# Attention and routed experts on one core: the low halves of the attention weights stored inside the float32 weights, eight steps deep, with new places for the side bank's users

## The chip, the cores and the metric

The kernel runs on one core of one Trainium2 chip. The metric is the device time in microseconds of one execution, shown as the median of three runs (2865.32 us, from 2861.77 to 2865.99).

## The reference

The input x has 4 sequences of 2048 tokens with 256 features, 8192 tokens in all. Cut to what matters, the reference is:

```
xn = layernorm(x)
s  = attention(xn)        # second norm with gain, 8 heads of 64, one shared K and V head,
                          # q and k scaled to norm 4, softmax(q k') v, Wout, norm with gain
g  = silu(experts(xn))    # router 256 -> 8, best 2, capacity 2560 rows an expert,
                          # gelu(x w1 + b1) w2 + b2, 1024 hidden, weighted sum of the two
out = x + s * g
```

Matrix products need more accuracy than one bf16 product gives. The kernel splits their operands into a high and a low half of 16 bits and adds the partial products that matter.

## The kernel before

**Groups and steps.** Queries are taken in 16 groups of 512 tokens, four groups to a sequence. A group's attention takes 64 steps. In a step TensorE computes the scores of two heads against 128 keys (six matmuls, L640, into one of two PSUM pairs of banks), ScalarE takes the exponential of the 128x1024 block (`exponent`, L869), and VectorE makes the low halves of the weights (`low`, L1220). TensorE then multiplies the weights with V, for the high halves (L668, 32 matmuls) and the low halves (L679, 16 matmuls).

**The product buffers.** `arena` holds NP = 6 float32 blocks (`p_f32`). The high half of a weight is the upper 16 bits of its float32 (`p_top[..., 1]`), read where it lies with a step of two elements. The low halves have six contiguous bf16 blocks of their own (`p_lo`). The exponential of step n waits until step n - NP has been weighed, and the weighing is placed LAG = 5 steps behind the scores, two steps at a time.

**Slots.** Every engine's program is made from one list of slots, each an attention step or a piece of another stage. In each slot an engine first issues its main instruction and then those of the "side chains", small programs that say at which slot each piece of theirs stands (`clock.at`). Engines run in order, so a place in that list is a place in each engine's queue. `base[g]` is the slot in which group g's attention starts. The order is written out by hand in the tables `S_...`, `KV_AT`, `Q_AT`, `O_...` and `C_AT`.

**Side chains in the attention stages.** For each group the kernel prepares q (four tiles, `prepare_q`), keys and values of a group of a later sequence (`prepare_kv`), the statistics and the router's logits (`statistics`), and projects the finished heads with Wout (four tiles, `project_out`). Their results on TensorE all go through one PSUM bank, the side bank `banks[3]`: `Ring.take` makes each user wait until the one before it has been read out. The output projection's result is read out by VectorE at L1173 (`s_rows`), q's by ScalarE (L815 and L818, the second frees the bank), keys' and values' by ScalarE at L800, the logits' by VectorE at L966.

**Places in a group of 64 slots.** q stands at 14, 30, 46 and 62, the projections at 37, 45, 53 and 61, keys and values at 38. The logits' place moves by 24 slots from one group to the next and so falls on 1, 9, 17, ... of a group of 64.

**Around the experts.** Eight groups come first, then all experts (L694 and L708), then the other eight groups. In these last ones `combine` gathers the experts' rows, multiplies and adds the result to `out` with a DMA from `res`.

SyncE issues the loads, stores and DMA transposes, in slot order too.

Of the kernel before, what the change touches and what calls it, by code (L numbers as in the profile page):

```python
# [7 lines left out]
F32 = mybir.dt.float32  # L8
# [7 lines left out]
P = 128  # L16
GT = 4
# [3 lines left out]
MIN_NORM = 1e-12  # L21
BANK = 512

NP = 6
LAG = 5
BEHIND = 4


# [41 lines left out]
def build_program(nc, x, norm_g, Wq, Wkv, Wout, out_norm_g, wr, w1, b1, w2, b2, out):  # L70
# [88 lines left out]
    def steps_to(g):  # L159
# [6 lines left out]


    S_SHIFT, S_NORM, S_HI, S_LO, S_STORE, S_TURN, S_LOGITS = [
        [early] * BG + [late] * (NG - BG) for early, late in ((3, 5), (4, 7), (5, 9), (6, 11), (9, 12), (9, 15), (12, 26))]
    KV_AT = [12 + 6 * g for g in range(BG)]  # L170
    KV_AT += [base[g - BG] + 38 for g in range(BG, NG)]

    EARLY_K_TURN, EARLY_Q_TURN = 9, 11
    Q_AT = [12 + 6 * j for j in range(GT)]
# [6 lines left out]
    for t in range(NT):  # L181
        g, j = divmod(t, GT)
        if g in BY_PE:
            at = experts_at + 4 * j if g == XG else place["post", 0, 0] + 1 + 6 * j
            O_SPLIT.append(at + 1)
            O_TURN.append(at + 4)
            O_PROJECT.append(at + 7)
        else:
            O_SPLIT.append(base[g + 1] + 11 + 4 * j)
            O_TURN.append(base[g + 1] + 27)  # L190
            O_PROJECT.append(base[g + 1] + 37 + 8 * j)
    C_AT = [base[XG + 1] + 20 + 13 * t if t < EARLY else O_SPLIT[t] + 8 if t // GT in BY_PE else
            base[t // GT + 1] + 34 + 12 * (t % GT) for t in range(NT)]
    C_ORDER = sorted(range(NT), key=lambda t: C_AT[t])
# [26 lines left out]
    with ExitStack() as ctx:  # L221
# [80 lines left out]


        PAIR = 2 * BANK
        arena = sb("arena", [P, NP * PAIR * 6], mybir.dt.uint8)
        p_f32 = arena[:, 0:NP * PAIR * 4].bitcast(F32).rearrange("p (n c) -> p n c", n=NP)
        p_top = arena[:, 0:NP * PAIR * 4].bitcast(BF16).rearrange("p (n c t) -> p n c t", n=NP, t=2)
        p_lo = arena[:, NP * PAIR * 4:NP * PAIR * 6].bitcast(BF16).rearrange("p (n c) -> p n c", n=NP)
        h_hi = [arena[:, i * 8192:(i + 1) * 8192].bitcast(BF16).rearrange("p (f c) -> p f c", f=FC) for i in (0, 1)]
        h_lo = [arena[:, i * 8192:(i + 1) * 8192].bitcast(BF16).rearrange("p (f c) -> p f c", f=FC) for i in (2, 3)]  # L310
        w1_hi = [sb(f"w1_hi{i}", [P, DC, F], BF16) for i in range(2)]
# [5 lines left out]
        xgT = [cut(flat(att[(XG + 1) % 2], F16), i, [2 * DC, GP]) for i in range(2)]  # L317
        b2_rows = [cut(flat(vhl_row[1], F32), i, [D]) for i in range(2)]

        res = [cut(flat(w1_lo[1], F32), i, [D]) for i in range(2)]  # L320
        y_got = [cut(flat(w1_lo[0], F32), i, [TOP_K, D]) for i in range(2)]

        early_x = [cut(flat(att[g // 2], F32), g % 2, [GT, D]) for g in range(BG)]
# [71 lines left out]
        c_loaded = [sem(f"c_loaded{i}") for i in range(2)]  # L395
        y_gathered = [sem(f"y_gathered{i}") for i in range(2)]
        x_copied = sem("x_copied")
        out_stored = [sem(f"out_stored{i}") for i in range(2)]
        f_first, f_both, c_tanh, c_silu, c_times = [sem(n) for n in (
            "f_first", "f_both", "c_tanh", "c_silu", "c_times")]  # L400

# [45 lines left out]
        def _(engine):  # L447
# [197 lines left out]
            def weigh(n, turn):  # L645

                s = n % NP
                if turn:
                    pe.wait_ge(half_weighed, n - n % 2 + 2)
                else:  # L650
                    pe.wait_ge(weighed, n - n % 2)
                pe.wait_ge(exped, n + 1)
                if n == CUT:
                    pe.wait_ge(y_done, FG * GT)
                for i, g, h, kb in halves(n):
                    b, hh = g // BG, g * H + h
                    V, bank = vhl[b % 2], acc_banks[hh % 3]
                    pe.wait_ge(v_split, BG * b + kb // GT + 1)
                    if kb == 0:
                        pe.wait_ge(divided, hh - 2)  # L660
                for qb in range(GT):
                    at = qb * (DH + 1)
                    for width, of in ((DH + 1, 0), (DH, DH + 1)):
                        for i, g, h, kb in halves(n):
                            V, bank = vhl[g // BG % 2], acc_banks[(g * H + h) % 3]
                            rows = slice((i + turn) % 2 * DH, ((i + turn) % 2 + 1) * DH)
                            cols = slice(i * BANK + qb * P, i * BANK + (qb + 1) * P)
                            nc.tensor.matmul(bank[:, at:at + width], p_top[rows, s, cols, 1],  # L668
                                             V[rows, kb, of:of + width],
                                             start=(kb == 0 and qb == 0 and turn == 0 and of == 0), stop=False,  # L670
                                             skip_group_check=True)
                pe.wait_ge(lowed, n + 1)
                for qb in range(GT):
                    at = qb * (DH + 1)
                    for i, g, h, kb in halves(n):
                        V, bank = vhl[g // BG % 2], acc_banks[(g * H + h) % 3]
                        rows = slice((i + turn) % 2 * DH, ((i + turn) % 2 + 1) * DH)
                        cols = slice(i * BANK + qb * P, i * BANK + (qb + 1) * P)
                        t = nc.tensor.matmul(bank[:, at:at + DH + 1], p_lo[rows, s, cols], V[rows, kb, 0:DH + 1],  # L679
                                             start=False, stop=(kb == KB - 1 and turn == 1), skip_group_check=True)  # L680
                t.then_inc(weighed if turn else half_weighed, 1)

# [56 lines left out]
        def _(engine):  # L739
# [68 lines left out]
            def prepare_q(t_id):  # L808
                g, j = divmod(t_id, GT)
                yield from clock.at(Q_AT[t_id])  # L810
                bank = where["q", t_id]
                act.wait_ge(q_projected, t_id + 1)
                act.wait_ge(q_scaled, t_id)
                act.wait_ge(s_rstd, g + 1)
                nc.scalar.activation(q_f[:, :, :].rearrange("p h n -> p (h n)"), bank, ACT.Copy,  # L815
                                     scale=rstd[:, g, 1, j:j + 1]).then_inc(q_copied, 1)
                act.wait_ge(q_lo, t_id)
                nc.scalar.activation(q_n[:, :, :].rearrange("p h n -> p (h n)"), bank, ACT.Square,  # L818
                                     scale=rstd[:, g, 1, j:j + 1]).then_inc(q_squared, 1)
                yield from clock.at(Q_AT[t_id] + 6)  # L820
                act.wait_ge(q_scaled, t_id + 1)
                act.wait_ge(q_turned_early, min(t_id, GT))
                act.wait_ge(q_stored, 16 * (t_id - GT) if t_id > GT else 0)
                cast(q_his, q_n[:, :, :].rearrange("p (a b) n -> p a b n", b=2)).then_inc(q_hi, 1)
                if t_id < GT:
                    yield from clock.at(Q_AT[t_id] + EARLY_Q_TURN)
                    act.wait_ge(q_turned_early, t_id + 1)
                    cast(qT[0][:, :, j * P:(j + 1) * P], where["qT", t_id].bitcast(F16).rearrange(
                        "p (h c) -> p h c", h=H)).then_inc(qT_copied, 1)
# [66 lines left out]
        def _(engine):  # L896
# [223 lines left out]
                                        ALU.subtract).then_inc(k_lo, 1)  # L1120

            def prepare_q(t_id):
                yield from clock.at(Q_AT[t_id] + 1)
                dve.wait_ge(q_squared, t_id + 1)
                nc.vector.tensor_reduce(q_small[:, 0, :], q_n[:, :, :], AX, ALU.add).then_inc(q_sum, 1)
                dve.wait_ge(q_sum, t_id + 1)
                nc.vector.tensor_scalar(q_small[:, 1, :], q_small[:, 0, :], SCALE ** 2 / (SCALE ** 3),  # L1127
                                        MIN_NORM ** 2 / SCALE ** 3, ALU.mult, ALU.max).then_inc(q_var, 1)
                yield from clock.at(Q_AT[t_id] + (5 if t_id < GT else 4))
                dve.wait_ge(q_rstd, t_id + 1)  # L1130
                nc.vector.tensor_tensor(q_n[:, :, :], q_f[:, :, :],
                                        q_small[:, 2, :].unsqueeze(2).to_broadcast([P, H, DH]),
                                        ALU.mult).then_inc(q_scaled, 1)
                yield from clock.at(Q_AT[t_id] + (7 if t_id < GT else 8))
                dve.wait_ge(q_hi, t_id + 1)
                nc.vector.tensor_tensor(q_los, q_n[:, :, :].rearrange("p (a b) n -> p a b n", b=2), q_his,
                                        ALU.subtract).then_inc(q_lo, 1)
# [38 lines left out]
            def combine(t_id):  # L1176
# [11 lines left out]
                if t_id < EARLY:  # L1188
# [1 line left out]
                dve.wait_ge(s_ready, t_id + 1)  # L1190
                dve.wait_ge(o_rstd, t_id + 1)
                dve.wait_ge(c_silu, i + 1)
                dve.wait_ge(out_stored[i % 2], 16 * (i // 2))
                nc.vector.scalar_tensor_tensor(out=res[i % 2], in0=w, scalar=half_rstd[:, t_id:t_id + 1], in1=s,
                                               op0=ALU.mult, op1=ALU.mult).then_inc(c_times, 1)

            def divide(hh):
# [18 lines left out]
            def low(n):  # L1216
                dve.wait_ge(exped, n + 1)
                dve.wait_ge(weighed, n - NP + 1)
                c = columns(n)
                nc.vector.tensor_tensor(p_lo[:, n % NP, c], p_f32[:, n % NP, c], p_top[:, n % NP, c, 1],  # L1220
                                        ALU.subtract).then_inc(lowed, 1)

            def rest_of_hidden(fg, f):
# [30 lines left out]
        def _(engine):  # L1254
# [49 lines left out]
                power(k_small[:, 2, :], k_small[:, 1, :], GT).then_inc(k_rstd, 1)  # L1304

            def prepare_q(t_id):
                yield from clock.at(Q_AT[t_id] + 2)
                pool.wait_ge(q_var, t_id + 1)
                power(q_small[:, 2, :], q_small[:, 1, :], H).then_inc(q_rstd, 1)

# [5 lines left out]
            def combine(t_id):  # L1316
# [12 lines left out]
                yield from clock.at(C_AT[t_id] + 15)  # L1329
                pool.wait_ge(x_copied, 16 * NG)  # L1330
                pool.wait_ge(c_times, i + 1)
                nc.gpsimd.dma_start(out_tiles[t_id], res[i % 2], accum_op=ALU.add).then_inc(out_stored[i % 2], 16)  # L1332

            def main(kind, a, b):
                pass
# [6 lines left out]
        def _(engine):  # L1342
# [48 lines left out]
            def prepare_kv(g):  # L1391
                b, gi = divmod(g, BG)
                if g < BG:
                    return
                yield from clock.at(KV_AT[g] - (34 if g > BG else 22))
                sp.wait_ge(s_stored[g % 2], 16 * (g // 2 + 1))
                sp.wait_ge(q_projected, GT * (g - BG + 1))
                sp.wait_ge(kv_projected, g)
# [16 lines left out]
            def prepare_q(t_id):  # L1415
                g, j = divmod(t_id, GT)
                if g == 0:
                    return
                yield from clock.at(Q_AT[t_id] + 9)
                sp.wait_ge(q_lo, t_id + 1)  # L1420
                nc.sync.dma_start(q_tiles[t_id], qhl[:, :, :, :, :].rearrange("p a k b n -> p (a k b n)")
                                  ).then_inc(q_stored, 16)
# [77 lines left out]
            def main(kind, a, b):  # L1500
# [5 lines left out]
                zero_rows(i) for i in range(NZERO)] + [move_rows(t) for t in range(NT)] + [load_routed(fg) for fg in range(FG)] + [project_out(t) for t in range(NT)] + [store_rows(fg) for fg in range(FG)] + [  # L1506
                copy_x(g) for g in range(NG)] + [
                combine(t) for t in C_ORDER])
            for i in range(2):
                sp.wait_ge(out_stored[i], 16 * NT // 2)  # L1510


_INS = ["L0_attn_x", "L0_attn_norm_g", "L0_attn_Wq", "L0_attn_Wkv", "L0_attn_Wout", "L0_attn_out_norm_g",
# [18 lines left out]
```

## Time and profile before

| | |
|---|---|
| median of 3 runs | 2865.32 us (2861.77 to 2865.99) |
| the profiled execution, its own time | 2859.94 us |
| its span, first to last instruction | 2858.2 us |
| TensorE matmuls busy | 2607.0 us, 91% of the span |
| VectorE busy | 2015.9 us, 71% |
| ScalarE busy | 1742.5 us, 61% |
| GpSimd busy | 673.4 us, 24% |
| mean granted TensorE clock | 0.976 |

Times in a view are from the span's start. The busy time of an engine counts its own instructions only. Idle time before an instruction is put down to what ended it; "issue" means that no semaphore explains it. The matmuls' ends are modelled, so that a busy TensorE is not one at its peak. Some matmul records are missing.

### The profile page before, as it was taken

How to read it: one execution, taken by the hardware profiler on the slowest of the kernel's cores; microseconds unless marked ns; L12 is line 12 of the kernel's file. 1: busy time of each engine (PE TensorE's matmuls, PEld its weight loads, DVE VectorE, ACT ScalarE, POOL GpSimd, SP SyncE). 2: the span in 40 equal slices, each digit the busy share in tenths (PEclk: the TensorE clock that was granted, in tenths of full speed). 3: DMA queues.
4: the chain of work that ended last, by engine and by line, in shares of the span. 5: the costliest groups of instructions: out<-in, count | busy, mean ns of one | idle time of the engine just before them, and what ended most of it. 6: DMA issues, size and time to landing. Idle time of an engine off the chain costs nothing. (4 is left out here: it accounts for less than half of the span.)

```text
span 2858.2 us, 136218 instructions
## 1 busy us (share of the span) xinstructions
PE 2607.0 (91%) x63045; PEld 1839.0 (64%) x63045; DVE 2015.9 (71%) x3013; ACT 1742.5 (61%) x2259; POOL 673.4 (24%) x492
## 2 busy tenths in 40 slices
PE   4898989888798999999999999999999899999995
PEld 3666666655466666666676666776666666666674
DVE  5888879889787874333433434348888899889985
ACT  6776757665565655554545545447766667667673
POOL 3111111111677500000000000003243434434313
PEclk8999999999899999999999999999999999999997
DMA  3455556322654522323323322211443434334412
GB/s 100 107 118 132 130 124 152 87 63 66 177 144 142 128 59 60 106 55 96 106 68 97 96 63 69 51 44 41 80 83 80 84 78 91 72 73 85 71 45 39
DMA packets 405611, 254.50 MB, mean 89 GB/s; under 512 B 291433, under 2 KB 369201, under 8 KB 404785
## 3 DMA queue, kind: packets, MB, share of 16 engines
q1 hardware_dynamic: 383536, 203.82, 29.4%
q0 software_dynamic: 21504, 41.96, 6.8%
q8 instruction: 494, 8.09, 1.2%
q14 instruction: 77, 0.62, 0.1%
HBM read 65.32 MB, written 121.63 MB: 65 GB/s over the span
## 5 line engine op out<-in xcount | busy, mean ns | idle before, releaser
L1220 DVE TENSOR_TENSOR arena<-arena 128x1024 bf16<-128x1024 f32 (+1 forms) x1032 | 1223.5, 1210 | 217.5 <-ACT arena L869 215.4
L869 ACT ACTIVATE arena<-pair 128x1024 f32<-128x1024 f32 (+1 forms) x1032 | 1041.6, 1016 | 419.5 <-PE pair L640 416.0
L668 PEld LDWEIGHTS bank<-vhl,arena 64*128 64x128 bf16 x32768 | 752.7, 95 | 288.5 <-issue 64.2
L640 PE MATMUL pair<-qT,kT 64*128 64x512 f16 x6144 | 864.3, 381 | 34.5 <-ACT arena L869 23.2
L668 PE MATMUL bank<-vhl,arena 64*128 64x64 bf16 (+1 forms) x32768 | 842.2, 191 | 44.8 <-issue 42.7
L679 PE MATMUL bank<-vhl,arena 64*128 64x65 bf16 x16384 | 616.4, 191 | 43.3 <-issue 27.8
L876 ACT ACTIVATE h_f<-pair,b1T 128x512 f32<-128x512 f32 x320 | 218.8, 684 | 379.6 <-PE pair L694 379.1
L679 PEld LDWEIGHTS bank<-vhl,arena 64*128 64x128 bf16 x16384 | 412.5, 95 | 54.9 <-issue 34.5
L1269 POOL TENSOR_TENSOR q_small<-q_small,minus_half 128x8 f32<-128x8 f32 x64 | 144.6, 2260 | 1272.7 <-DVE q_small L1127 1272.3
L708 PE MATMUL bank<-w_hl,arena 128*128 128x256 bf16 x3840 | 426.9, 273 | 0.3
L708 PEld LDWEIGHTS bank<-w_hl,arena 128*128 128x128 bf16 x3840 | 375.3, 98 | 53.6 <-DVE att L1236 2.0
L1226 DVE TENSOR_TENSOR arena<-h_f,arena 128x512 bf16<-128x512 f32 x320 | 221.4, 692 | 264.7 <-ACT arena L743 264.1
L694 PE MATMUL pair<-att,w_hi 128*128 128x512 f16 x1280 | 382.6, 381 | 2.5 <-DMA att<-routed_rows 2.5
L640 PEld LDWEIGHTS pair<-qT,kT 64*128 64x128 f16 x6144 | 247.2, 94 | 211.9 <-issue 66.7
L1236 DVE TENSOR_TENSOR att<-bank,vhl 128x256 f32<-128x256 f32 x160 | 67.8, 424 | 263.4 <-PE bank L708 261.9
L694 PE MATMUL pair<-att,w_lo 128*128 128x512 f16 x640 | 243.6, 381 | 0.0
L694 PEld LDWEIGHTS pair<-att,w_hi 128*128 128x128 bf16 x1280 | 125.4, 98 | 145.5 <-DMA att<-routed_rows 2.7
L743 ACT ACTIVATE arena<-h_f 128x512 bf16<-128x512 f32 x320 | 201.5, 630 | 10.1
L1325 POOL DMA_INDIRECT w_lo<-expert_rows,gather_from x128 | 186.7, 1458 | 81.4 <-DVE c_work L1182 50.8
L1297 POOL DMA_INDIRECT routed_rows<-xT_out,scatter_to x128 | 168.8, 1319 | 83.2 <-issue 32.4
L815 ACT ACTIVATE q_f<-bank,rstd 128x512 f32<-128x512 f32 x63 | 43.3, 688 | 129.9 <-PE bank L566 129.5
L1269 POOL TENSOR_TENSOR half_rstd<-o_small,minus_half 128x1 f32<-128x1 f32 x64 | 39.6, 618 | 349.3 <-DVE o_small L1165 349.0
(190 smaller groups left out, 1596.5 us busy)
## 6 DMA issues: line engine op xcount, KB each, us to landing
routed_rows<-h_f SPq DMA_DIRECT2D x80, 256.0 KB
expert_rows<-att SPq DMA_DIRECT2D x40, 512.0 KB, 2.8
raw<-in_L_ffn_w SPq DMA_DIRECT2D x32, 512.0 KB, 4.6
q_rows<-qhl SPq DMA_DIRECT2D x60, 256.0 KB
o_rows<-o_hl SPq DMA_DIRECT2D x56, 256.0 KB
xn_rows<-s_hl SPq DMA_DIRECT2D x16, 512.0 KB, 3.3
xT_out<-xn_rows SPq DMA_DIRECT2D x64, 128.0 KB
out<-in_L_attn_x SPq DMA_DIRECT2D x16, 512.0 KB, 4.2
```

Source lines behind the costliest of these rows:

```text
L640: t = nc.tensor.matmul(into, kT[g // BG % 2][rows, k_part, keys], qT[g % 2][rows, h // 2 * 2 + q_part, :], start=(k_part + q_part == 0), s ...
L668: nc.tensor.matmul(bank[:, at:at + width], p_top[rows, s, cols, 1], V[rows, kb, of:of + width], start=(kb == 0 and qb == 0 and turn == 0 a ...
L679: t = nc.tensor.matmul(bank[:, at:at + DH + 1], p_lo[rows, s, cols], V[rows, kb, 0:DH + 1], start=False, stop=(kb == KB - 1 and turn == 1) ...
L694: t = nc.tensor.matmul(bank, w[e % 2][:, c, cols], xgT[fg % 2][:, kind, :], start=(n == 0), stop=(n == 3 * DC - 1))
L708: t = nc.tensor.matmul(bank[:, 0:D], h[fg % 2][:, f, cols], w2_hl[e % 2][:, f, at:at + D], start=(f == 0 and h is h_hi and at == 0), stop= ...
L743: return nc.scalar.activation(o, i, ACT.Copy)
L869: nc.scalar.activation(p_f32[:, n % NP, columns(n)], pairs[n % 2][:, columns(n)], ACT.Exp).then_inc(exped, 1)
L876: nc.scalar.activation(h_f32[k % 2], lent[k % 4], ACT.Gelu_apprx_tanh, bias=b1T[:, e * FC + f:e * FC + f + 1]).then_inc(gelued, 1)
L1220: nc.vector.tensor_tensor(p_lo[:, n % NP, c], p_f32[:, n % NP, c], p_top[:, n % NP, c, 1], ALU.subtract).then_inc(lowed, 1)
L1226: nc.vector.tensor_tensor(h_lo[fg % 2][:, f, :], h_f32[k % 2], h_hi[fg % 2][:, f, :], ALU.subtract).then_inc(h_rest, 1)
L1269: return nc.gpsimd.tensor_tensor(o, i, minus_half[:, 0:n], ALU.pow)
L1325: nc.gpsimd.indirect_dma_start(y_got[i % 2][:, k, :], None, expert_rows, bass.IndirectOffsetOnAxis(gather_from[k][:, t_id:t_id + 1], 0)).t ...
```

## The change

Seven edits are made together.

1. `p_lo` is gone. `low` writes the low half of each weight into the lower 16 bits of the weight's own float32 (`p_top[..., 0]`), and the low-half matmuls read it there, with a step of two elements.
2. NP goes from 6 to 8 and LAG from 5 to 7.
3. The side bank's users move: keys and values from slot 38 of the group to 22, the last three projections from 45, 53 and 61 to 40, 53 and 56, the logits two slots later.
4. In `prepare_q` ScalarE makes its second read of the bank (the square) one slot later than the first, and the steps on VectorE, GpSimd and SyncE behind it follow one slot later.
5. SyncE issues the load of xT for keys and values at slot 2 of the group, and not at 4.
6. `res` has four buffers and four semaphores in place of two.
7. With LAG, each of the two attention stages gets two more slots, in which only weighing is left, and the weighing starts two slots later.

```diff
-NP = 6
-LAG = 5
+NP = 8
+LAG = 7
...
-        [early] * BG + [late] * (NG - BG) for early, late in ((3, 5), (4, 7), (5, 9), (6, 11), (9, 12), (9, 15), (12, 26))]
+        [early] * BG + [late] * (NG - BG) for early, late in ((3, 5), (4, 7), (5, 9), (6, 11), (9, 12), (9, 15), (12, 28))]
...
-    KV_AT += [base[g - BG] + 38 for g in range(BG, NG)]
+    KV_AT += [base[g - BG] + 22 for g in range(BG, NG)]
...
-            O_PROJECT.append(base[g + 1] + 37 + 8 * j)
+            O_PROJECT.append(base[g + 1] + (37, 40, 53, 56)[j])
...
-        arena = sb("arena", [P, NP * PAIR * 6], mybir.dt.uint8)
+        arena = sb("arena", [P, NP * PAIR * 4], mybir.dt.uint8)
...
-        p_lo = arena[:, NP * PAIR * 4:NP * PAIR * 6].bitcast(BF16).rearrange("p (n c) -> p n c", n=NP)
...
-        res = [cut(flat(w1_lo[1], F32), i, [D]) for i in range(2)]
+        res = [cut(flat(w1_lo[1], F32), i, [D]) for i in range(4)]
...
-        out_stored = [sem(f"out_stored{i}") for i in range(2)]
+        out_stored = [sem(f"out_stored{i}") for i in range(4)]
...
-                        t = nc.tensor.matmul(bank[:, at:at + DH + 1], p_lo[rows, s, cols], V[rows, kb, 0:DH + 1],
+                        t = nc.tensor.matmul(bank[:, at:at + DH + 1], p_top[rows, s, cols, 0], V[rows, kb, 0:DH + 1],
...
+                if g:
+                    yield
...
-                yield from clock.at(Q_AT[t_id] + 6)
+                yield from clock.at(Q_AT[t_id] + (6 if g == 0 else 7))
...
-                yield from clock.at(Q_AT[t_id] + 1)
+                yield from clock.at(Q_AT[t_id] + (1 if t_id < GT else 2))
...
-                yield from clock.at(Q_AT[t_id] + (5 if t_id < GT else 4))
+                yield from clock.at(Q_AT[t_id] + 5)
...
-                yield from clock.at(Q_AT[t_id] + (7 if t_id < GT else 8))
+                yield from clock.at(Q_AT[t_id] + (7 if t_id < GT else 9))
...
-                dve.wait_ge(out_stored[i % 2], 16 * (i // 2))
-                nc.vector.scalar_tensor_tensor(out=res[i % 2], in0=w, scalar=half_rstd[:, t_id:t_id + 1], in1=s,
+                dve.wait_ge(out_stored[i % 4], 16 * (i // 4))
+                nc.vector.scalar_tensor_tensor(out=res[i % 4], in0=w, scalar=half_rstd[:, t_id:t_id + 1], in1=s,
...
-                nc.vector.tensor_tensor(p_lo[:, n % NP, c], p_f32[:, n % NP, c], p_top[:, n % NP, c, 1],
+
+                nc.vector.tensor_tensor(p_top[:, n % NP, c, 0], p_f32[:, n % NP, c], p_top[:, n % NP, c, 1],
...
-                yield from clock.at(Q_AT[t_id] + 2)
+                yield from clock.at(Q_AT[t_id] + (2 if t_id < GT else 3))
...
-                nc.gpsimd.dma_start(out_tiles[t_id], res[i % 2], accum_op=ALU.add).then_inc(out_stored[i % 2], 16)
+                nc.gpsimd.dma_start(out_tiles[t_id], res[i % 4], accum_op=ALU.add).then_inc(out_stored[i % 4], 16)
...
-                yield from clock.at(KV_AT[g] - (34 if g > BG else 22))
+                yield from clock.at(base[g - BG] + (2 if g > BG else 16))
...
-                yield from clock.at(Q_AT[t_id] + 9)
+                yield from clock.at(Q_AT[t_id] + 10)
...
-            for i in range(2):
-                sp.wait_ge(out_stored[i], 16 * NT // 2)
+            for i in range(4):
+                sp.wait_ge(out_stored[i], 16 * NT // 4)
```

## Rows read from the trace of the kernel before

**Rows 1.** Busy time by stretch: before, during and after the experts

```profile
core 0: us, PE busy (x) PEld busy (x) DVE busy (x) ACT busy (x) POOL busy (x), PEclk, DMA share, GB/s
67.00:1059.00 992.00, 874.33 (x28527) 627.68 (x28526) 833.03 (x1218) 635.09 (x742) 309.44 (x212) 0.97 0.47 116
1059.00:1912.00 853.00, 848.37 (x5890) 572.21 (x5887) 322.27 (x527) 432.80 (x671) 2.15 (x4) 1.00 0.28 76
1912.00:2812.00 900.00, 836.45 (x28153) 603.38 (x28152) 804.77 (x1102) 622.38 (x760) 323.77 (x238) 0.99 0.36 73
```

**Rows 2.** TensorE's waits: waiter, releaser, us in total, times, longest

```profile
PE bank L668 <- issue: 42.7, 64, 3.0
PE bank L566 <- DVE s_rows L1173: 38.8, 19, 5.6
PE bank L679 <- issue: 27.8, 44, 1.4
PE pair L640 <- ACT arena L869: 23.2, 28, 9.6
PE bank L679 <- DVE arena L1220: 14.5, 29, 1.7
PE bank L534 <- DVE s_rows L1173: 8.8, 6, 2.3
...
PE bank L601 <- DVE s_rows L1173: 1.7, 2, 1.0
PE bank L511 <- DVE s_rows L1173: 1.3, 1, 1.3
```

**Rows 3.** Timeline around a projection and the q behind it

```profile
2328.85 1.48 PE L617 MATMUL bank<-wo_hl,att 128*128 128x256 bf16 x12
...
2333.68 0.47 DVE L1173 SCALAR_TENSOR_TENSOR s_rows<-bank,o_small,out_g 128x256 f32<-128x256 f32 x1
...
2334.22 0.81 PE L566 MATMUL bank<-wq_hi,xT 128*128 128x512 bf16 x2 [2.39 <-DVE s_rows L1173]
...
2336.67 1.41 PE L640 MATMUL pair<-qT,kT 64*128 64x512 f16 x6
```

**Rows 4.** Ten stretches at half clock: the first, the last, their sum

```profile
269.40:272.80 3.40, 3.09 (x10) 0.50 0.84 192
...
2477.80:2481.20 3.40, 3.40 (x36) 0.51 0.68 142
sum 37.40, PE 35.46; mean PE 3.55
```

**Rows 5.** Timeline: the scores of two steps in a row, undisturbed

```profile
402.24 0.82 PE L640 MATMUL pair<-qT,kT 64*128 64x512 f16 x6
...
403.63 0.81 PE L640 MATMUL pair<-qT,kT 64*128 64x512 f16 x6
```

**Rows 6.** Groups of instructions: busy us, mean ns of one, idle before

```profile
L1220 DVE TENSOR_TENSOR arena<-arena 128x1024 bf16<-128x1024 f32 (+1 forms) x1032 | 1223.5, 1210 | 217.5 <-ACT arena L869 215.4 <-PE bank L679 0.4 <-issue 0.3
L869 ACT ACTIVATE arena<-pair 128x1024 f32<-128x1024 f32 (+1 forms) x1032 | 1041.6, 1016 | 419.5 <-PE pair L640 416.0
...
L668 PEld LDWEIGHTS bank<-vhl,arena 64*128 64x128 bf16 x32768 | 752.7, 95 | 288.5 <-issue 64.2 <-PE bank L679 4.4
...
L679 PEld LDWEIGHTS bank<-vhl,arena 64*128 64x128 bf16 x16384 | 412.5, 95 | 54.9 <-issue 34.5 <-DVE arena L1220 18.8
...
L1194 DVE SCALAR_TENSOR_TENSOR w_lo<-c_work,half_rstd,s_xin 128x256 f32<-128x256 f32 x32 | 15.5, 485 | 3.5 <-DVE c_work L1186 1.0
...
L1046 DVE TENSOR_TENSOR w_hl<-w_hl,w_lo 128x512 f32<-128x512 f32 x1 | 0.7, 678 | 0.0
```

**Rows 7.** Busy time by stretch: the groups 10 and 14

```profile
2132.50:2251.20 118.70, 107.44 (x3566) 77.10 (x3560) 105.52 (x152) 80.36 (x104) 48.76 (x36) 0.99 0.44 85
...
2597.00:2705.60 108.60, 102.29 (x3520) 73.88 (x3514) 101.60 (x142) 77.63 (x96) 47.37 (x34) 1.00 0.37 72
```

**Rows 8.** The page's DMA queues: packets, MB, share of 16 engines

```profile
q8 instruction: 494, 8.09, 1.2%
```

**Rows 9.** ScalarE's waits: the two longest that VectorE ended

```profile
ACT c_work L860 <- DVE c_work L1182: 42.4, 34, 4.7
ACT qhl L743 <- DVE q_n L1131: 28.6, 28, 3.6
```

## The prediction

> **What bounds the kernel now.** I read the busy time by stretch first. The experts (853 us) keep TensorE busy for 848.37 us, and no edit touches their work. The two attention stretches, 992 and 900 us, are where the change acts. TensorE is busy there for 874.33 and 836.45 us, VectorE for 833.03 and 804.77 us, ScalarE for little over 620 to 635 us [rows 1]. So TensorE leads, VectorE follows closely, and ScalarE has room.
>
> An undisturbed step takes 1.39 us, from one step's first score matmul to the next one's [rows 5]. VectorE needs 1.21 us of it for the low halves and ScalarE 1.02 us for the exponential [rows 6]. 64 such steps are 89 us, while group 14 took 108.6 us and group 10 118.7 us [rows 7]: the rest is side work and waits.
>
> The waits of TensorE are the next view [rows 2]. The side bank is waited for until VectorE has read out a projection: 38.8 + 8.8 + 1.7 + 1.3 = 50.6 us. "issue" takes 42.7 + 27.8 = 70.5 us. Waits for low halves take 14.5 us, for exponentials 23.2 us. The timeline shows how one side bank wait arises: the projection's matmuls end at 2330.33 us, VectorE works through older work in its queue and ends the read-out at 2334.15 us, and q's matmuls, one slot behind, start at 2334.22 after 2.39 us idle [rows 3].
>
> Such a wait costs a second time. Right behind it q's six matmuls take from 2334.22 to 2336.67, 2.45 us, and the scores after them show 1.41 us where 0.82 is usual [rows 3, 5]. I looked for stretches at half clock and for what stood at their start: ten of them, 37.4 us together, stand at a side bank wait, with a granted clock of 0.5, the lower of the two levels (1.2 and 2.4 GHz) [rows 4].
>
> **Part by part.**
>
> *The side bank's users (edit 3).* A wait of this kind is on average 38.8 / 19 = 2.0 us, behind a slot of 1.39 us, so the bank is free some 3.4 us after the projection's last matmul. Where one slot lay between a projection and its successor (45 to 46, 61 to 62, 37 to 38), now at least three lie there (40 to 46, 56 to 62, 37 to 40), 4.2 us. The average fits, the longest (5.6 + 1.39 = 7.0 us) does not. New neighbours three slots apart (37 and 40, 53 and 56) can wait too. I leave 6 us and take -44.6. Bounds: -50.6, all gone, and -25, half of it comes back at the new neighbours. Keys and values leave slot 38; their nine VectorE instructions stood at 39 and 43, just ahead of the read-out at 45, and now stand at 23 and 27, where none waits behind them. That is in the same term.
>
> *The clock.* Half speed for 37.4 us loses at most 18.7 us. In [rows 3] the loss was 2.45 us against about 1.28 (half) for q alone. Some of it lay where ScalarE or VectorE were late anyway. I take -13, with bounds 0 and -18.7. The Trainium skill (TensorE: Matmul & The Clock Gate, HAM oscillation) reckons throttled time times one half, which gives 18.7 us here and a sum 6 us lower; the trace agrees with the half speed itself, since q's matmuls took twice as long.
>
> *Eight deep, seven behind (edit 2).* The distance from an exponential to the step that frees its buffer is one slot more than LAG before and after, so ScalarE gains nothing. VectorE does: a low half may be two slots later before TensorE waits. What that can return is the 14.5 us of waits for low halves [rows 2]. I take half, -7, bounds 0 and -14.5. The 23.2 us for exponentials stay, since ScalarE's distance is the same as before.
>
> *Low halves in place (edit 1).* The instruction count is the same. TensorE loads weights with a step of two elements already for the high halves: 95 ns, and 95 ns for the contiguous low halves [rows 6]. So the loads cost 0. VectorE's write is new: bf16 with a step of two, over its own input. Nearest row below: an in-place f32 TENSOR_TENSOR, 678 ns for 512 [rows 6], which continues to 1210 for 1024 at 1.04 ns an element, the present rate; so nothing more. Nearest above: the slowest VectorE form per element, 485 ns for 256; less the same fixed 146 ns it is 1.32 ns an element, 0.29 us more for 1024. I take 0, because a float32 write steps over the same bytes at the usual rate. Both ends stay for the range.
>
> *Longer fill and drain (edit 7).* Two more steps in two stages have only scores on TensorE (0.82 us) while VectorE sets 1.21 us: 4 x 0.4 = 1.6 us, rounded to +2, bounds 0 and 4. The weighing left over at the ends is work moved, not added.
>
> *q's chain (edit 4)* adds no instruction. The bank is held one slot longer, and the next user stands two or more slots away. Behind ScalarE's square wait VectorE's reduction, GpSimd's power and SyncE's store, all one slot later. SyncE's eight transposes of qT stay at slot 58 and q's last store moves to 56, still eight slots ahead of the next group. 0. *xT's load and keys (edits 3, 5)*: SyncE issues four transposes two slots earlier, the k store at 29 and the two kT transposes at 32 of the group, right behind the eight of the projection at 27, where before they stood at 45 and 48. They queue; the projection at 37 could be late by a DMA. The bytes are the same, K is needed groups later. 0, bounds 0 and +5. *Four res buffers (edit 6)*: no wait of VectorE names the store, so 0.
>
> *What is late next.* TensorE without pauses draws instructions faster, and VectorE must keep up. Part of the "issue" time comes back: 70.5 us over about 1,900 us of attention is 3.7%; where 31 side bank waits covered such a delay, I put +5 (0 to +15). VectorE: after the change the attention would last about 1892 - 52 = 1840 us with 1637.8 us busy [rows 1], 89%. Group 14 ran at 101.6 of 108.6, 93.6%, with little waiting [rows 7]; so it can, but in the crowded groups (10: 105.5 busy, floor 105.5 / 0.936 = 112.7 us against the 111 I would hope for) some comes back: +6 (0 to +20).
>
> *Sum*: -44.6 - 13 - 7 + 2 + 5 + 6 = -51.6 us. The profiled execution took 2859.94 us, 5.4 less than the median of 2865.32; 2859.9 - 51.6 = 2808.3 in its terms, and about 2814 in those of the median.
>
> **The rivals.**
>
> *A, forecast:* the pauses go and most of it is kept, 2790 to 2835. Chance 0.52.
>
> *B, VectorE takes the place.* The waits move from the side bank to low halves and to ScalarE, which already waits for VectorE for 42.4 + 28.6 us [rows 9]; a deeper buffer lets VectorE fall further behind and makes these longer. For it: VectorE is at 105.5 of 118.7 us in group 10. Against it: only 14.5 us of waits for low halves now. If crowding costs 30 us in place of 6 and the clock returns half, the sum is about -21: 2844. Chance 0.17.
>
> *C, instructions take the place.* TensorE gets its instructions in 494 packets, 8.09 MB, with the other engines' [rows 8]; each "issue" wait stands inside a run of matmuls that wait for no semaphore. If 25 of the 50 us come back there, with the clock's gain halved, it is about -25: 2840. Chance 0.07. The Trainium skill (Runtime: NRT & Kernel Launch, Instruction fetch mechanics) holds this fetch to be mostly hidden, by which this rival would have no room; the 70.5 us of this trace speak against it.
>
> *D, slower: the strided write.* At +0.29 us VectorE is busy for 1032 x 0.29 = 299 us more, 1937 us in attention, above its present 1892 us; at the 93.6% of group 14 it needs 2069 us. Between them lies about +110 us: 2975. It decides from 1840 x 0.936 = 1722, so (1722 - 1638) / 1032 = 0.08 us a step. A smaller slowing, or a transposing queue on SyncE that makes projections late in every group, ends nearer. Chance 0.12, over all of that.
>
> *E, more:* low-half waits, clock and side bank give all they hold and the rows behind absorb it: -50.6 - 18.7 - 14.5 + 2 = -82: 2784 and below. Chance 0.09. *F, nothing:* what is saved at one bank user is waited for at the next: within 0.2%. Chance 0.03.
>
> **How the numbers follow.** 0.2% of the time, 5.7 us, is about what a measurement of this kernel can tell from no change. Faster by more: A, C, E and nearly all of B, 0.84. Within: F and the ends of B and D, 0.05. Slower: the rest of D, 0.11. The range 2775 to 2850 holds A, most of B and C, and the near part of E, and leaves D out; A's own is 2790 to 2835.
>
> **What would show it.** Side bank waits on `s_rows` under 10 us in all; fewer stretches at half clock, mean clock from 0.976 to about 0.983; low halves still at 1.21 us; waits for low halves under 15 us; "issue" between 70 and 85 us; group 10 near 111 us and group 14 unchanged near 108; TensorE busy less by what the clock gives. The prediction fails if the low halves take over 1.29 us, if ScalarE's waits for VectorE double, or if the waits reappear at 37 to 40 and 53 to 56.

## The result

The changed kernel takes 2959.68 us (median of 4 runs, 2953.06 to 2968.85), the kernel before 2865.65 us beside it: a ratio of 1.033, 95% interval 1.0294 to 1.0365. It is slower by 3.3%, where 1.8% faster was forecast. The profiled execution has a span of 2962.4 us; the mean granted clock fell from 0.976 to 0.964.

Busy time by stretch of the changed kernel, before, during and after the experts, with columns as in [rows 1]:

```profile
67.00:1127.00 1060.00, 884.55 (x28441) 628.76 (x28441) 890.35 (x1216) 638.03 (x742) 466.48 (x212) 0.94 0.45 109
1127.00:1983.00 856.00, 850.96 (x5985) 574.60 (x5978) 322.56 (x528) 432.66 (x671) 2.16 (x4) 1.00 0.28 76
1983.00:2914.00 931.00, 837.07 (x28099) 603.12 (x28098) 865.89 (x1103) 620.48 (x761) 530.87 (x238) 0.99 0.36 70
```

The experts are as they were. The two attention stretches are longer by 68 and 31 us. TensorE and ScalarE have the same instructions. VectorE is busy for 118 us more, now more than TensorE in both stretches, and GpSimd is busy for 997 us where it was 633.

Groups of instructions of the changed kernel that answer to [rows 6] (L1222 was L1220). L1271 is GpSimd's power for q, which raises the squared lengths to the power of -0.5; L1327 is the gather of the experts' rows in `combine`:

```profile
L1222 DVE TENSOR_TENSOR arena<-arena 128x1024 bf16<-128x1024 f32 (+1 forms) x1032 | 1358.1, 1365 | 82.8 <-ACT arena L870 80.6
...
L667 PEld LDWEIGHTS bank<-vhl,arena 64*128 64x128 bf16 x32768 | 750.8, 95 | 291.4 <-issue 63.5
...
L1271 POOL TENSOR_TENSOR q_small<-q_small,minus_half 128x8 f32<-128x8 f32 x64 | 233.1, 3642 | 1259.7 <-DVE q_small L1128 1259.5
...
L678 PEld LDWEIGHTS bank<-vhl,arena 64*128 64x128 bf16 x16384 | 412.1, 95 | 37.8 <-issue 35.9
...
L1327 POOL DMA_INDIRECT w_lo<-expert_rows,gather_from x128 | 336.1, 2626 | 78.7 <-DVE c_work L1183 48.7
```

A low half takes 1365 ns, not 1210. (Both are means over 1032 instructions, 16 of which have 512 elements; those of 1024 alone take 1374 and 1219 ns.) Loading the weights with a step of two costs nothing, 95 ns as before. Unforeseen is GpSimd: its power for q takes 3642 ns, its gathers 2626. In the kernel before these two groups, and VectorE's wait for the power, were:

```profile
L1269 POOL TENSOR_TENSOR q_small<-q_small,minus_half 128x8 f32<-128x8 f32 x64 | 144.6, 2260 | 1272.7 <-DVE q_small L1127 1272.3
L1325 POOL DMA_INDIRECT w_lo<-expert_rows,gather_from x128 | 186.7, 1458 | 81.4 <-DVE c_work L1182 50.8 <-issue 30.7
```

```profile
DVE q_n L1131 <- POOL q_small L1269: 10.1, 8, 3.8
```

TensorE's waits in the changed kernel, against [rows 2]:

```profile
PE pair L639 <- ACT arena L870: 138.4, 92, 11.6
PE bank L667 <- issue: 36.4, 56, 1.9
PE bank L678 <- issue: 30.3, 42, 1.8
PE bank L616 <- DMA att<-o_rows: 26.9, 7, 14.3
PE pair L639 <- DMA qT<-q_rows: 13.1, 7, 5.6
...
PE bank L616 <- DVE s_rows L1174: 8.2, 12, 1.4
...
PE bank L678 <- DVE arena L1222: 0.7, 2, 0.4
```

The side bank waits are nearly gone, as forecast (8.2 us in this row, about 12 in all), and so are those for low halves. In their place the scores wait 138.4 us for exponentials, and the waits for DMAs grow from 12.6 to 40.0 us (26.9 and 13.1 here; 10.6 and 2.0 before). The new places alone don't make the latter: with them and contiguous low halves (experiment 6) they are 15.8 us. Who holds ScalarE, and who holds VectorE behind it, the waits of these two engines tell (against [rows 9]):

```profile
ACT qhl L742 <- DVE q_n L1132: 143.1, 55, 13.9
...
ACT c_work L861 <- DVE c_work L1183: 60.9, 41, 4.7
ACT o_hl L742 <- DVE att L1214: 39.0, 14, 6.4
```

```profile
DVE q_n L1132 <- POOL q_small L1271: 120.2, 41, 13.9
DVE arena L1222 <- ACT arena L870: 80.6, 66, 5.2
```

So there is a chain: VectorE waits for GpSimd's power, ScalarE for VectorE's scaled q, the next exponential stands behind that in ScalarE's queue, and TensorE waits for it. One link of it in the changed kernel's timeline:

```profile
2067.22 0.17 DVE L1128 TENSOR_SCALAR q_small<-q_small 128x8 f32<-128x8 f32 x1
2067.30 3.90 DVE L1222 TENSOR_TENSOR arena<-arena 128x1024 bf16<-128x1024 f32 x3
2067.48 5.22 POOL L1271 TENSOR_TENSOR q_small<-q_small,minus_half 128x8 f32<-128x8 f32 x1 [0.88 <-DVE q_small L1128]
...
2072.74 0.69 DVE L1132 TENSOR_TENSOR q_n<-q_f,q_small 128x512 f32<-128x512 f32 x1 [1.53 <-POOL q_small L1271]
...
2073.46 0.63 ACT L742 ACTIVATE qhl<-q_n 128x512 f16<-128x512 f32 x1 [1.93 <-DVE q_n L1132]
```

While three low halves run back to back for 3.90 us, the power, started at 2067.48, doesn't end; it ends at 2072.70, 1.5 us after the last of them, and VectorE stands idle for that time. It is as if the power got on only once VectorE paused.

Groups 10 and 14 (against [rows 7]), and the groups 5 and 6, in which GpSimd scatters the rows and which took 139.1 and 124.6 us before:

```profile
2209.10:2331.50 122.40, 107.32 (x3564) 76.61 (x3558) 112.89 (x152) 79.79 (x103) 69.70 (x36) 0.99 0.41 81
2687.50:2802.30 114.80, 103.94 (x3538) 74.89 (x3532) 108.70 (x142) 77.35 (x95) 70.56 (x33) 0.99 0.34 72
```

```profile
678.30:839.00 160.70, 113.75 (x3556) 80.28 (x3551) 124.75 (x169) 81.76 (x93) 113.98 (x51) 0.89 0.42 115
839.00:995.20 156.20, 113.72 (x3560) 80.83 (x3556) 103.41 (x125) 75.02 (x84) 135.57 (x75) 0.88 0.43 122
```

The groups 5 and 6 alone lose 53 us, and there it is for the most part not the power's own length. Of VectorE's 120.2 us of waits for it, 73.0 us are eight waits of over 4 us, all between 760 and 1047 us, six of them in these two groups, and each time the power itself took 1.7 us. It started late, because GpSimd's queue had fallen behind with scatters (1955 ns on average against 1319 before, the longest 10.05 us against 2.00). The end of the longest of these waits:

```profile
888.90 0.96 POOL L1299 DMA_INDIRECT routed_rows<-xT_out,scatter_to  x1 [0.31 <-issue]
889.88 1.68 POOL L1271 TENSOR_TENSOR q_small<-q_small,minus_half 128x8 f32<-128x8 f32 x1
...
891.59 0.69 DVE L1132 TENSOR_TENSOR q_n<-q_f,q_small 128x512 f32<-128x512 f32 x1 [13.91 <-POOL q_small L1271]
```

From 878.77 us on, with VectorE idle, GpSimd issues nine scatters of 0.96 us each, and only then comes to the power. Beside low halves just before, they took up to 5.88 us. So the chain has two causes in GpSimd, a slow power and slow scatters and gathers ahead of it.

### The profile page after: what moved, and what is told of

Same layout as the page of the kernel before. It is cut to its first block and busy times, and to the rows that moved or that the text cites. A ratio compares the mean times of both kernels' runs of the same rounds, so it can differ in the third digit from the quotient of the medians.

```text
span 2962.4 us, 136209 instructions
## 1 busy us (share of the span) xinstructions
PE 2621.8 (89%) x63045; PEld 1843.5 (62%) x63045; DVE 2134.2 (72%) x3013; ACT 1743.4 (59%) x2259; POOL 1037.4 (35%) x492
## 5 line engine op out<-in xcount | busy, mean ns | idle before, releaser
L1222 DVE TENSOR_TENSOR arena<-arena 128x1024 bf16<-128x1024 f32 (+1 forms) x1032 | 1358.1, 1365 | 82.8 <-ACT arena L870 80.6
L639 PE MATMUL pair<-qT,kT 64*128 64x512 f16 x6144 | 867.4, 384 | 156.3 <-ACT arena L870 138.4
L1271 POOL TENSOR_TENSOR q_small<-q_small,minus_half 128x8 f32<-128x8 f32 x64 | 233.1, 3642 | 1259.7 <-DVE q_small L1128 1259.5
L1327 POOL DMA_INDIRECT w_lo<-expert_rows,gather_from x128 | 336.1, 2626 | 78.7 <-DVE c_work L1183 48.7
L1299 POOL DMA_INDIRECT routed_rows<-xT_out,scatter_to x128 | 250.2, 1955 | 70.5 <-ACT arena L870 33.6
L1271 POOL TENSOR_TENSOR half_rstd<-o_small,minus_half 128x1 f32<-128x1 f32 x64 | 57.9, 905 | 250.2 <-DVE o_small L1166 249.9
L1132 DVE TENSOR_TENSOR q_n<-q_f,q_small 128x512 f32<-128x512 f32 x64 | 44.3, 692 | 120.3 <-POOL q_small L1271 120.2
```

What stands on the lines that cost most here:

```text
L639: t = nc.tensor.matmul(into, kT[g // BG % 2][rows, k_part, keys], qT[g % 2][rows, h // 2 * 2 + q_part, :], start=(k_part + q_part == 0), s ...
L1222: nc.vector.tensor_tensor(p_top[:, n % NP, c, 0], p_f32[:, n % NP, c], p_top[:, n % NP, c, 1], ALU.subtract).then_inc(lowed, 1)
L1271: return nc.gpsimd.tensor_tensor(o, i, minus_half[:, 0:n], ALU.pow)
L1299: nc.gpsimd.indirect_dma_start(routed_rows, bass.IndirectOffsetOnAxis(scatter_to[k][:, t:t + 1], 0), moving[t % 4], None).then_inc(rows_sc ...
L1327: nc.gpsimd.indirect_dma_start(y_got[i % 2][:, k, :], None, expert_rows, bass.IndirectOffsetOnAxis(gather_from[k][:, t_id:t_id + 1], 0)).t ...
```

## The experiments

Ratios are to the kernel before on the same chip. "P" and the other letters are the theories that each text names.

**1. The write in place alone, and all but the write.** The first puts edit 1 into the kernel before:

```diff
-nc.vector.tensor_tensor(p_lo[:, n % NP, c], p_f32[:, n % NP, c], p_top[:, n % NP, c, 1], ...
+nc.vector.tensor_tensor(p_top[:, n % NP, c, 0], p_f32[:, n % NP, c], p_top[:, n % NP, c, 1], ...
```

> The kernel before with edit 1 alone: low halves written into the float32 weights, still six buffers and five steps behind, every place as before. Theory P (the price of the low halves carries the loss): VectorE's low halves take 1.36 to 1.37 us in place of 1.21, VectorE is busy for some 118 us more, and without the side bank's gain the time is 2950 to 3020 us. Rival Q (the moved places and the deeper lag carry the loss, by SyncE's and GpSimd's queues; the longer low halves lie in VectorE's slack): the low halves take 1.36 us too, but the time stays within 2865 to 2890 us.

Measured: 3010.53 us, ratio 1.052 (1.0477 to 1.0562). Low halves 1361 ns, GpSimd's power 2999 ns, side bank waits 88.3 us in all where they were 50.6. The group of low halves and that of the power:

```profile
L1219 DVE TENSOR_TENSOR arena<-arena 128x1024 bf16<-128x1024 f32 (+1 forms) x1032 | 1360.8, 1361 | 170.1 <-ACT arena L868 163.3 <-issue 6.2
...
L1268 POOL TENSOR_TENSOR q_small<-q_small,minus_half 128x8 f32<-128x8 f32 x64 | 191.9, 2999 | 1220.4 <-DVE q_small L1126 1220.2
```

The second takes edit 1 out of the changed kernel. Eight buffers with contiguous blocks beside them would need 12 KiB more in each partition, so NP and LAG go back as well:

```diff
-NP = 8
-LAG = 7
+NP = 6
+LAG = 5
-nc.vector.tensor_tensor(p_top[:, n % NP, c, 0], ...
+nc.vector.tensor_tensor(p_lo[:, n % NP, c], ...
```

> The changed kernel with the low halves back in contiguous blocks of their own, and so with six buffers and five steps behind; the side bank's places, q's chain, the loads and the four res buffers as changed. Theory P: low halves at 1.21 us, side bank waits under 15 us, 2800 to 2840 us, faster than before by 1 to 2%. Rival Q: 2880 us or more, with the exponentials late (over 100 us of waits of the score matmuls for them) as in the changed kernel.

Measured: 2826.14 us, ratio 0.9866 (0.9823 to 0.991), low halves 1211 ns, the power 2254 ns. Theory P holds: edit 1 carries the loss, the rest is a gain. Q falls. That NP and LAG went back too doesn't blur this: the six-deep kernel of experiment 5 (1.035) differs from this one in edit 1 alone.

**2. Is it the step, or writing over the input?** Both kernels have NP = 4 and LAG = 3, which leaves room to write the low halves with a step of two into a region of their own:

```diff
-nc.vector.tensor_tensor(p_lo[:, n % NP, c], p_f32[:, n % NP, c], ...
+nc.vector.tensor_tensor(p_two[:, n % NP, c, 0], p_f32[:, n % NP, c], ...
```

> The kernel before with four buffers and three steps behind, contiguous low halves: the partner of the next run, which needs more room a buffer. Only the duration of the low halves matters: 1.21 us. With less depth TensorE waits more for low halves; 2870 to 2960 us.

> As the run before it, four buffers and three steps behind, but the low halves are written with a step of two elements into a region of their own, not into their inputs. If the step is what costs, 1.36 us as in the changed kernel, and a time above its partner's by 60 us or more. If writing into the words that the same instruction reads is what costs, 1.21 us and its partner's time within 10 us. A value between says that both have a part.

Measured, one run each: 3007.98 us with contiguous low halves, 3114.22 us with the step. The group of low halves, first contiguous, then with the step:

```profile
L1220 DVE TENSOR_TENSOR arena<-arena 128x1024 bf16<-128x1024 f32 (+1 forms) x1032 | 1240.7, 1214 | 359.1 <-ACT arena L869 351.1 <-PE bank L679 3.5 <-issue 1.7
```

```profile
L1220 DVE TENSOR_TENSOR arena<-arena 128x1024 bf16<-128x1024 f32 (+1 forms) x1032 | 1384.3, 1361 | 321.2 <-ACT arena L869 315.6 <-PE bank L679 2.6 <-issue 0.5
```

1214 and 1361 ns: the step costs all of it, and writing over the input nothing. Four buffers were slower than expected (3008 us, outside the 2870 to 2960): TensorE then waits 279.5 us for low halves.

**3. VectorE's time, or GpSimd's turn?** Contiguous low halves cut into parts make VectorE as busy as the step does.

```diff
-nc.vector.tensor_tensor(p_lo[:, n % NP, c], p_f32[:, n % NP, c], ..., ALU.subtract).then_inc(lowed, 1)
+for at in range(c.start, c.stop, BANK):      # in the three-part kernel: 512, 256, 256
+    h = slice(at, at + BANK)
+    t = nc.vector.tensor_tensor(p_lo[:, n % NP, h], p_f32[:, n % NP, h], ..., ALU.subtract)
+t.then_inc(lowed, 1)
```

> The kernel before with each contiguous low-half instruction of 1024 cut into two of 512, which took 0.693 us each where they occur: 1.39 us a step, slightly more than the 1.36 us of the write with a step of two, and with no such write. Theory T (VectorE's time alone makes the loss): 3000 to 3040 us, close to the 3010.5 us of the in-place write in the same kernel, and GpSimd's power for q goes from 2.26 us towards 3 us too. Rival U (the write with a step of two harms others beside its own length, GpSimd above all): 2900 to 2960 us, and the power stays near 2.3 us.

Measured: 2888.75 us, ratio 1.0083 (1.0052 to 1.0113). Both ranges missed, for it wasn't the clean test that the text says: the two parts overlap at their ends, so that VectorE was busy with low halves for 1292.4 us, 0.067 us a step more, not 0.18. GpSimd's power took 2000 ns. The next run corrects the size:

> The kernel before with each contiguous low-half instruction cut into three, of 512, 256 and 256. Two parts added 0.067 us a step to VectorE's busy time (1.292 in place of 1.224 ms in all), so three add some 0.134 us and VectorE is as busy as with the write in place (about 2135 us), but GpSimd can take its turn between the parts. If VectorE's time alone made the loss of the in-place write (3010.5 us), this ends near 2990 to 3020 us. If GpSimd's turns made a good part of it, 2900 to 2940 us, with the power for q near 2.0 us.

Measured: 2923.81 us, ratio 1.0181 (1.0147 to 1.0214), low halves busy 1357.5 us as with the step, the power 1989 ns. VectorE's time by itself costs 1.8%, while the step in the same kernel costs 5.2%. The gathers took 1502 ns here, against 2747 with the step.

The other way round, the in-place low halves of experiment 1 cut in two:

> The kernel with the in-place write alone (3010.5 us), its low-half instruction cut into two of 512. VectorE works longer, by about 0.067 us a step, 69 us in all, and GpSimd gets a turn between the two. If VectorE's time is what counts, 3050 to 3080 us. If GpSimd being kept out is what counts, the time falls although VectorE has more to do: 2940 to 2990 us, and the power for q falls from 3.0 us to about 2.2.

Measured: 2943.35 us, ratio 1.0231 (1.0195 to 1.0267). Its low halves and its power for q:

```profile
L1221 DVE TENSOR_TENSOR arena<-arena 128x512 bf16<-128x512 f32 x2048 | 1367.7, 746 | 179.2 <-ACT arena L868 173.7 <-issue 4.8
...
L1271 POOL TENSOR_TENSOR q_small<-q_small,minus_half 128x8 f32<-128x8 f32 x64 | 127.0, 1984 | 1267.6 <-DVE q_small L1126 1267.5
```

VectorE is as busy as uncut (1367.7 against 1360.8 us; no 69 us more), the power falls from 2999 to 1984 ns, and the time from 1.052 to 1.023. That is where contiguous parts with the same VectorE time stand (1.018; the intervals overlap). VectorE is busy for 71 to 73% of the span in all these kernels, and also with contiguous low halves in one piece, where the power takes 2275 ns (places alone, experiment 6). So neither the busy time nor the step alone makes the power slow, but a stepped write in one long piece. The gathers are another matter: cut in two they still take 2284 ns, so that the step has a part of its own in them.

**4. GpSimd out of q's chain.** In the changed kernel:

```diff
+nc.vector.reciprocal(q_small[:, 2, :], q_small[:, 1, :]).then_inc(q_rstd, 1)
-power(q_small[:, 2, :], q_small[:, 1, :], H).then_inc(q_rstd, 1)
```

> The changed kernel without GpSimd's power in q's chain: VectorE takes a reciprocal there, so that q is scaled by one over its squared length and not by one over the length. It costs VectorE 64 x 0.18 = 12 us and takes the wait for GpSimd (120 us in the changed kernel) out of its queue. If that wait carries the loss, 2890 to 2925 us, with waits of the score matmuls for exponentials under 70 us (138 in the changed kernel). If VectorE's own time carries it, 2960 to 2975 us.

Measured: 2902.1 us, ratio 1.0109 (1.0082 to 1.0137), against 1.033 with the power. The scores wait 76.4 us for exponentials (somewhat over the 70 forecast), not 138.4. The link counts, though gathers (2753 ns) and the other powers stay slow. The edit takes VectorE's wait away whichever its cause, the slow power or the scatters ahead of it, so it doesn't weigh the two.

**5. Time for q's chain, and the depth.** Two runs on the changed kernel. The first gives the steps behind the power two slots more:

```diff
-yield from clock.at(Q_AT[t_id] + 5)
+yield from clock.at(Q_AT[t_id] + (5 if t_id < GT else 7))
```

> The changed kernel with the steps of q behind GpSimd's power two slots later (VectorE's scaling at 7, ScalarE's cast at 9, VectorE's rest at 11, the store at 12, the transposes at 13). VectorE waited for that power 120 us in the changed kernel. If these waits cost time by themselves, they fall under 40 us and the time to 2900 to 2930 us. If GpSimd only gets its turn when VectorE pauses, the power takes longer instead and the time stays within 10 us of 2960 us.

Measured: 2968.76 us, ratio 1.036 (1.0328 to 1.0391). VectorE's wait for the power fell to 58.6 us, but the power took 4069 ns. The scores waited less for exponentials (93.2 us) and more for the transposes of qT (41.2 us against 13.1), and the side bank's users 27.6 us for read-outs against 11.6. Room at this place doesn't help, since what it saves is waited for elsewhere.

> The changed kernel with six buffers and five steps behind, low halves still in place. It tells what the two buffers more give once VectorE is the bound. Theory: depth lets VectorE fall behind without TensorE waiting for low halves, so this is slower than the changed kernel by 10 to 30 us, 2970 to 2990 us, with 40 us or more of waits for low halves. Rival: depth only moves the waits from the low halves to the exponentials, the same within 6 us of 2960 us.

Measured: 2963.36 us, ratio 1.035 (1.0314 to 1.0386), against 1.033 (1.0294 to 1.0365) with eight: no difference that these runs can tell. Waits for low halves are 66.3 us and not 0.7, those for exponentials 107.1 and not 138.4: the rival's reading, the depth mostly moves the wait.

**6. The places alone, and the changed kernel with cut low halves.** The first puts only the side bank's places into the kernel before (the load of xT stays at slot 4):

```diff
-(12, 26)
+(12, 28)
-KV_AT += [base[g - BG] + 38 ...
+KV_AT += [base[g - BG] + 22 ...
-O_PROJECT.append(base[g + 1] + 37 + 8 * j)
+O_PROJECT.append(base[g + 1] + (37, 40, 53, 56)[j])
```

> The kernel before with the side bank's places alone: keys and values at 22, projections at 37, 40, 53 and 56, logits two slots later; q's chain, xT's load at slot 4, two res buffers, six deep as before. Theory: the places carry all of the gain seen with everything but the in-place write (2826 us): 2820 to 2835 us. Rival: ScalarE's later square (q's chain) has a part, then 2840 to 2855 us.

Measured: 2815.49 us, ratio 0.982 (0.9786 to 0.9853), the fastest of all. The whole of TensorE's waits for the side bank after a projection:

```profile
PE bank L601 <- DVE s_rows L1173: 1.7, 2, 1.0
...
PE pair L640 <- DVE s_rows L1173: 1.4, 1, 1.4
PE bank L617 <- DVE s_rows L1173: 0.3, 1, 0.3
```

Against 2826.14 us with q's chain, xT's load and four res buffers as well, the intervals of the two ratios overlap; these other edits give nothing that the runs can tell.

> The changed kernel with its in-place low halves cut into two instructions of 512. Cut in the kernel with the in-place write alone, VectorE was as busy as before (1368 against 1361 us in the low halves) and the time fell by 67 us. If the same mechanism makes the changed kernel slow, 2880 to 2910 us, GpSimd's power for q near 2.0 us and VectorE's wait for it under 20 us (120 in the changed kernel). If the moved places or the depth make it slow, 2950 us or more. Even at best it stays above the places alone (2815 us), since VectorE still has 0.13 us a step more to do.

Measured over 10 runs: 2877.28 us, ratio 1.0025 (0.9997 to 1.0053), the power 1939 ns, waits for exponentials 78.1 us. VectorE's wait for the power is 31.7 us, not under 20; nearly all of it (30.7 us) comes with a power that started right behind another instruction of GpSimd, the longest four behind scatters. One more instruction in each step brings the changed kernel back to the time of the kernel before. Against the places alone (0.982) it is still 2 points slower, so it takes back some 60% of what the step costs.

## Why the prediction was wrong

**The step that failed** is "Low halves in place (edit 1)": "I take 0, because a float32 write steps over the same bytes at the usual rate." The run measured 1365 ns, 0.155 us more a step, or 0.13 us in VectorE's busy time (1358.1 against 1223.5 us). The bracket of 0 to 0.29 us held it, and rival D had the right place: it decides from 0.08 us a step, and both are beyond. My own sign of failure, low halves of over 1.29 us, is what came. Two things were wrong in my use of that bracket. The nearer row was no row of such a write at all: the in-place f32 instruction has the overlap but not the step, and experiment 2 shows that the overlap is free and the step is what costs. And D had a chance of 0.12 only. With nothing like the operation in the trace, the middle of the bracket (0.14 us) lay far beyond the point of decision. The Trainium skill (SBUF — State Buffer, the cachelines note under Door 1) asks for two hits to a 16-byte line for full bandwidth; a bf16 step of two elements makes four and would be free by that. TensorE's reads here agree (95 ns both), VectorE's write doesn't.

**D's price lacked a term.** It counted VectorE's time alone. By its own floor the 1756 us that VectorE was busy in the two stretches need 1756 / 0.936 = 1876 us, less than the 1892 before; they took 1991. By experiment 3 VectorE's time costs +1.8%, and most of the rest up to +5.2% goes when the low halves are cut in two with VectorE equally busy. The text under "q's chain (edit 4)" named GpSimd's power among the steps and gave 0 for the chain; that the power itself could take longer, or start late behind slower scatters and gathers in GpSimd's queue, stood nowhere. The Trainium skill (SBUF — State Buffer, SBUF: two separate sides) says that of a VectorE instruction with two SBUF inputs and a GpSimd instruction that reads SBUF the one that starts first blocks the other for its whole length. The trace agrees in kind, with 5.22 us for a power beside three unbroken low halves, but the power got no turn between them either. Why GpSimd gets its turn at once between two parts of 512 (2.0 us) and so late between two whole ones, no run settles.

**The side bank (edit 3)** was right: waits from 50.6 to 3.4 us, and a gain of 1.8% or some 51 us (42 to 61; the two medians beside each other differ by 46), for which I had 44.6 + 13 less 11 to come back. Rival B's fear that VectorE would take it all back doesn't hold at 1.21 us a low half: in the places-alone kernel group 10 takes 114.5 us and group 14 110.6 (118.7 and 108.6 before), where I hoped for 111 and 108. That its 2815.5 us is close to the 2814 of the sum for the whole change is in part luck, since the sum has terms (-7 and +2) for edits that this kernel doesn't have. In the kernel with the in-place write the places, with q's chain, the load and res, give as much: 1.052 to 1.035.

**Rival C** ("issue" waits grow): 79 us in the places-alone kernel against 70.5 for the weighing, and 10.5 us more at q's matmuls (L566), where all the waits that the view of before shows were for the side bank. With all lines counted they grow from 77.8 to 95.6 us, more than the +5 of the sum and beyond its bound of +15.

**Depth** was put at -7 us. It can't be shown: with the write in place it is 0 within the error, and with contiguous low halves eight deep wasn't tried. **Fill and drain, res, xT's load**: too small to be told apart.

**The clock**: I expected 0.983; the places alone gave 0.980, the changed kernel 0.964. Read in windows of 1.7 us, about 160 us of it lie at half clock, against about 90 before. More of these stretches stand at waits for exponentials than at any other wait, such as one at 2054 us behind a wait of 4.8 us; a few stand at waits for a DMA.

## What to carry to other kernels

Before a store is moved into a stepped layout to save room, time that store on the engine that has least room; a row that shares only one of its two new features is no price for it. An engine that was 87% busy in these stretches (1638 of 1892 us) covers only part of 11% more of its main instruction: of the 134 us that three contiguous parts add to VectorE, some 52 reach the time. And where a small operation of GpSimd stands in a chain, look at how long VectorE's unbroken two-input instructions are beside it, and at what stands ahead of it in GpSimd's own queue. Here the places of the side bank alone are the version to keep (0.982), and in a kernel that must write with the step, cutting the instruction in two gives back a little over half of what the step costs (1.052 to 1.023, and 1.033 to 1.0025 where 0.982 is the time without it).

## What the runs showed of the hardware

- VectorE's low halves (128x1024, inputs f32 and bf16, output bf16; means with 16 of 512 among the 1032) take 1361 to 1368 ns written with a step of two elements, against 1210 to 1214 contiguous. Writing over the input adds nothing. The stepped read by TensorE's weight load costs nothing (95 ns both).
- GpSimd's 128x8 power takes 2.0 us beside VectorE instructions of 512 elements, 2.3 us beside contiguous ones of 1024, and 2.5 to 4.1 us on average beside stepped ones of 1024. It is least, 2.5 us, with four buffers, where VectorE has the most pauses; what sets it between 3.0 and 4.1 us no run settles.
- GpSimd's gathers take 1.4 to 1.5 us on average beside contiguous low halves, cut or not, 1.8 to 2.9 us beside stepped ones, and still 2.2 to 2.3 us where these are cut in two. Scatters took 0.96 us each while VectorE was idle, and up to 10.05 us beside stepped low halves.
- Cutting an instruction of 1024 in two costs 0.067 us of VectorE's busy time when the write is contiguous (1292.4 against 1223.5 us for all steps) and 0.007 us when it has the step (1367.7 against 1360.8).
